# A decoder layer on one core: V's remainder and the router's logits ahead of the moments, the norm behind the maxima's copy, and one product less

## The chip, the cores and the metric

The kernel runs on one core of a Trainium2 chip. The metric is the device time of one execution in microseconds (us), the median of several runs. The core has five engines that work side by side, each through its own instructions in a fixed order: TensorE (PE; its weight loads are listed as PEld), VectorE (DVE), ScalarE (ACT), GpSimd (POOL) and SyncE (SP, which here issues the DMAs). They wait for each other by semaphores only.

## What is computed

A post-norm decoder layer over 128 sequences of 64 tokens of width 128, with 16 heads of 8. The core of the reference:

```python
x = layernorm(x + retention(x))            # decayed scores, no softmax, gate, norm
x = layernorm(x + cross_attention(x, ctx)) # softmax over 64 context rows
o = causal_self_attention(x)               # softmax over the earlier tokens
h = layernorm(x + o @ w_o, g1, b1)
probs = softmax(h @ wg)                    # router over 8 experts
topv, topi = top_k(probs, 2)
y = layernorm(h + sum of the two chosen experts' gelu MLPs, g2, b2)
```

## The kernel before

The 8192 tokens are 64 tiles of 128 rows (two sequences each), and four tiles make a group. Each group goes through the three attentions one after the other, so there are 48 groups in one stream, numbered g: 0 to 15 are retention, 16 to 22 are cross-attention, then self-attention (odd g) and cross-attention (even g) alternate up to 41, and 42 to 47 are self-attention. Groups from 16 on are the "later groups" of the change.

The program is written out slot by slot. Slot s belongs to group g = s // 4 with k = s % 4, and in every slot `pe_slot`, `act_slot`, `pool_slot` and `dve_slot` append what each engine has to do. That order is final, so an instruction that waits holds up all behind it on its engine. In one slot the engines serve groups of several ages. With g the group that the slot is named for:

- k = 2 and k = 3 project K and Q of g (L546, L549) into `bankA`. ACT copies them as `kh` (L670) and `qh` (L677), and DVE keeps the remainders `kl` and `ql` (L820). ACT also spreads `kh` into eight key blocks `Kz` (L686), four at k = 2 and four at k = 3.
- k = 3 computes V of g in `bankB` (L622). ACT copies it to half precision, `Vh` (L699, `act_values`), and DVE takes the remainder `Vl` (L832, `dve_values`). Before the change both stand at k = 0 of the next group.
- In every slot PE makes scores for one tile in row order (L449, L464), from which DVE takes the maximum of each row, `mx` (L814), and scores for an older tile in column order (L449, L486), of which ACT takes the exponential, `P` (L725). POOL computes the rounding remainder `Plo` (L766), and PE sums P with V (L509 to L511). In every second slot DVE divides the sums by the denominators and stores `O` (L851, L863).
- k = 0: "the maxima's turn". PE turns the maxima of g - 2 with four small products into `bankB` (L592), ahead of which stands `pe_keep_clock(bankB, 1)`, a 128x512 product of no use (L442). ACT copies the turned maxima out, `mT` (L706, `act_maxima`, written at k = 1).
- k = 1: PE turns `O` of g - 4 in the same `bankB` (L516). k = 2: ACT copies it (`OT`, L714) and PE multiplies it by the output weights (L611). k = 3: DVE adds the residual (L883).
- The norm at the end of a group: DVE takes the moments `st` and `mv` (L870, L874), POOL makes `rstd` and `nmr` of them (L772 to L777, `pool_rescale`), and ACT scales the rows (L731, `act_normalise`). For a self-attention group the moments are taken at k = 3 of the fourth group after it, and `pool_rescale` and `act_normalise` stand at k = 0 of the fifth. DVE then applies g1 and b1 (L888, L890, `dve_affine`), and the router reads the rows from the sixth group on: `dve_router` (L904, L908) frees `bankA` for the K projection. POOL sends the routed rows out by indirect DMA (L784), two per slot.

PE may not begin to turn `O` until `mT` is copied, since both use `bankB`:

```python
if begun(g - 2) and kind(g - 2) != "ret":
    pe.wait_ge(*f_mTs(softmaxed(g - 2)))
```

The functions that the diff touches, and those that call them:

Of the kernel before, what the change touches and what calls it, by code (L numbers as in the profile page):

```python
# [104 lines left out]
def build(nc, x, xt, ctxt, wmats, cols, rows, const_ident, const_masks, const_ids, const_tri, const_rev, const_steps, const_blocks, const_region, const_pads, const_rows, wg, w1, bb1t, w2, bb2, out):  # L105
# [214 lines left out]
    LS, LT, LP = 5, 10, 12  # L320
# [38 lines left out]
    def softmaxed(g):  # L359

        return g - NG
# [5 lines left out]
    def begun(g):  # L367
        return 0 <= g < GROUPS

    def last(g):  # L370
        return begun(g) and kind(g) == "self"
# [66 lines left out]
    def pe_keep_clock(o, times):  # L438


        for _ in range(times):
            pe.matmul(o, ident[:, :], W[:, 0:4, :].rearrange("p w n -> p (w n)")[:, 0:o.shape[1]], start=True, stop=True)  # L442
# [139 lines left out]
    def pe_second(g, k):  # L582


        if k == 0 and begun(g - 2) and kind(g - 2) != "ret":
            m = softmaxed(g - 2)
            pe.wait_ge(*(f_Vl(g - 1) if begun(g - 1) else f_r(g - 5)))
            pe.wait_ge(*f_mTs(m - 1))
            pe_keep_clock(bankB, 1)
            pe.wait_ge(*f_max(GT * m + GT - 1))  # L590
            for t in range(GT):
                i = pe.matmul(bankB[0:32, t * P:(t + 1) * P], mx[m % 2][:, t, :], ident16[:, :], start=True, stop=True)  # L592
            i.then_inc(f_mT.of(m), 1)
        if k == 1 and begun(g - 4):
            if begun(g - 1):
                pe.wait_ge(*(f_V32 if kind(g - 1) == "ret" else f_Vl)(g - 1))
            else:
                pe.wait_ge(*f_r(g - 5))
            if begun(g - 2) and kind(g - 2) != "ret":
                pe.wait_ge(*f_mTs(softmaxed(g - 2)))  # L600
            if kind(g - 4) == "ret":
                pe.wait_ge(*f_On(g - 4))
            else:
                pe.wait_ge(*f_O(2 * (g - 4) + 1))
            pe_turn(bankB, O[g % 2]).then_inc(f_OT.of(g - 4), 1)
        if k == 2 and begun(g - 4):
            pe.wait_ge(*f_OTs(g - 4))
            if kind(g - 4) == "ret":
                pe.wait_ge(*f_OTg(g - 4))
            for t in range(GT):  # L610
                i = pe.matmul(bankB[:, t * P:(t + 1) * P], OT[g % 2][:, t * P:(t + 1) * P], weights_of(g - 4)["O"],  # L611
                              start=True, stop=True)
            i.then_inc(f_out.of(g - 4), 1)
        if k == 3 and begun(g):
            if begun(g - 1):
                pe.wait_ge(*f_Vl(g - 1))
            if begun(g - 2) and kind(g - 2) != "ret":
                pe.wait_ge(*f_mTs(softmaxed(g - 2)))
            if begun(g - 4):
                pe.wait_ge(*f_r(g - 4))  # L620
            for t in range(GT):
                i = pe.matmul(bankB[:, t * P:(t + 1) * P], source_of(g)[:, t * P:(t + 1) * P], weights_of(g)["V"],  # L622
                              start=True, stop=True)
            i.then_inc(f_V.of(g), 1)
# [55 lines left out]
    def act_key_blocks(g, slots):  # L680
        m = softmaxed(g)
        if m >= 2:
            act.wait_ge(*f_S(GT * (m - 2) + GT - 1))
        act.wait_ge(*f_kh(g))
        for slot in slots:
            i = act.activation(Kz[g % 2][:, slot, :], kh[g % 2][:, :], ACT.Identity, scale=column(f"slot{slot}"))  # L686
        return i
# [45 lines left out]

    def act_slot(s):
        g, k = s // GT, s % GT
        if k == 0 and begun(g - 1):
            act_values(g - 1)
        if k == 1 and begun(g - 2) and kind(g - 2) != "ret":
            act_maxima(g - 2)
        if k == 2 and begun(g - 4):  # L740
            act_turned(g - 4)
        if k == 1 and CHOSEN.get(g, NG) < NG:
            act_turned_rows(CHOSEN[g])
        if begun(g):
            act_first(g, k)
        if NG * GT <= s - LT < TILES:
            act_weights(s - LT)
        if 0 <= s - LP < NG * GT and (s - LP) % 2:
            results(act, s - LP)
        if k == 2 and begun(g) and kind(g) != "ret":  # L750
            act_key_blocks(g, range(0, 4))
        if k == 3 and begun(g) and kind(g) != "ret":
            act_key_blocks(g, range(4, 8)).then_inc(f_Kz.of(softmaxed(g)), 1)
        if k == 0 and begun(g - 4) and kind(g - 4) == "ret":
            act_normalise(0, g - 4, O[g % 2]).then_inc(f_On.of(g - 4), 1)
        if k == 0 and begun(g - 6) and not last(g - 6):
            act_normalise(1, g - 6, tiles_of(g - 6)).then_inc(f_y.of(g - 6), 1)
        if k == 0 and last(g - 5):
            act_normalise(1, g - 5, tiles_of(g - 5)).then_inc(f_y.of(g - 5), 1)


# [25 lines left out]
    def pool_slot(s):  # L787
        g, k = s // GT, s % GT
        if k == 1 and begun(g) and kind(g) != "self":
            pool.wait_ge(*(l_x(g) if kind(g) == "ret" else f_xT(softmaxed(g))))  # L790
            pool.tensor_tensor(tiles_of(g), tiles_of(g), brow("a_bo" if kind(g) == "ret" else "x_bo"), ALU.add).then_inc(f_xb.of(unmasked(g)), 1)
        if k == 2 and begun(g - 4) and kind(g - 4) == "ret":
            pool.wait_ge(*f_OTs(g - 4))
            pool.tensor_tensor(OT[g % 2][:, :], OT[g % 2][:, :], gate[(g - 4) % 5][:, :], ALU.mult).then_inc(f_OTg.of(g - 4), 1)
        if k == 0 and last(g - 5):
            pool_rescale(1, g - 5)
        if k == 0 and begun(g - 4) and kind(g - 4) == "ret":
            pool_rescale(0, g - 4)
        if 0 <= s - LT < TILES:
            pool_low(s - LT)  # L800
        if k == 2 and begun(g - 5) and not last(g - 5):
            pool_rescale(1, g - 5)
        if s in PLACED:
            pool_dispatch(*PLACED[s])
# [137 lines left out]

    def dve_slot(s):
        g, k = s // GT, s % GT
        if k == 0 and begun(g - 1) and kind(g - 1) != "ret":
            dve_values(g - 1)
        if k == 3 and begun(g - 4):
            dve_residual(g - 4)
        if NG * GT <= s - LS < TILES:
# [8 lines left out]
            dve_low(g, f_kh, l_K(g - 2), kl, kh, {"ret": "a_bk", "cross": "x_bk", "self": "k_zero"}[kind(g)], f_kl)  # L958
        if NG * GT <= s - LP < TILES and (s - LP) % 2:
            results(dve, s - LP)  # L960

        if k == 1 and begun(g - 5) and not last(g - 5):
            dve.wait_ge(*f_r(g - 5))
# [6 lines left out]
            dve_scalars(0, g - 3, O[(g - 3) % 2])  # L970
        if s == GT * AT["self", 0]:
            dve_routing_constants()
        if k == 1 and last(g - 5) and s - LP < TILES:
            dve_affine(g - 5)
        if k == 1 and g in CHOSEN:
            dve_router(CHOSEN[g])
        if k == 1 and last(g - 5) and s - LP >= TILES:
            dve_affine(g - 5)
        if k == 2 and CHOSEN.get(g, NG) < NG:
            dve_choose(CHOSEN[g], 0)  # L980
        if k == 0 and CHOSEN.get(g - 1, NG) < NG:
            dve_choose(CHOSEN[g - 1], 1)

# [520 lines left out]
```

## Time and profile before

| | |
|---|---|
| median of three runs | 1338.22 us (1336.91 to 1345.8) |
| profiled execution | 1334.23 us, its span 1332.9 us |
| retention alone, 0 to 240 us | PE busy 190.65 us |
| later groups, 240 to 874 us | PE busy 535.23, DVE 463.85, ACT 463.06, POOL 422.92 us |
| experts and the rest, 874 us to the end | PE busy 346.79 us |
| TensorE clock, 240 to 874 us | 0.87 of full |

The span begins with the first instruction in the trace and ends with the last; the profiled execution's own time is 1.3 us more. All times on the trace are counted from the start of the span. The clock column is a share of full speed: 1.00 is the level of 2.4 GHz all the time, 0.50 is 1.2 GHz all the time. In a timeline row the brackets at the end give how long the engine sat idle before the row and what ended that. "issue" stands there where the profile shows no releaser.

### The profile page before, as it was taken

To read this page: it belongs to the slowest core of one execution; us is meant where nothing else is said; L and a number is where in the kernel's file an instruction comes from. 1 tells how busy PE (TensorE), PEld (TensorE's weight loads), DVE (VectorE), ACT (ScalarE), POOL (GpSimd) and SP (SyncE) were. 2 spreads that over 40 slices of the span, in tenths; PEclk is the share of its full clock that TensorE was granted. 3 is DMA by queue.
4 is the path that set the end of the run, shared out by engine and by line. 5 is a ranking of instruction groups with operands and counts; after the bars stand their busy time and mean duration, and the time that the engine had idled before them with its cause. 6 is when DMAs were issued, how large, how long until landed. Compare 5 with 4: busy or idle time off the path is not lost.

```text
span 1332.9 us, 45920 instructions
## 1 busy us (share of the span) xinstructions
PE 1072.7 (80%) x17677; PEld 758.1 (57%) x17677; DVE 891.3 (67%) x2322; ACT 821.9 (62%) x1884; POOL 911.8 (68%) x859
## 2 busy tenths in 40 slices
PE   5888888889898887887887788867788799999552
PEld 2555555545555554554554455546777789989210
DVE  4776767767877887677775676755445467666475
ACT  2455555788989876767766675424445456666366
POOL 4888888776666557766666665875657656667576
PEclk9998999888999988889987898758889899999776
DMA  5464332212222222222221212111212233332353
GB/s 159 128 188 144 86 82 75 58 49 73 77 81 79 67 66 71 69 59 58 81 69 50 74 37 68 49 39 42 57 55 69 61 88 105 97 95 67 119 166 103
DMA packets 132182, 108.61 MB, mean 81 GB/s; under 512 B 19564, under 2 KB 122477, under 8 KB 131933
## 3 DMA queue, kind: packets, MB, share of 16 engines
q1 hardware_dynamic: 123548, 88.29, 24.2%
q0 software_dynamic: 8416, 17.38, 4.0%
q8 instruction: 141, 2.31, 0.8%
q14 instruction: 77, 0.62, 0.2%
HBM read 41.58 MB, written 26.75 MB: 51 GB/s over the span
## 4 chain that ended last, share of the span: by engine, by line
PE 44%; ACT 17%; issue 13%; DVE 13%; DMA 5%; POOL 3%; SPq 2%; another core or an unknown queue 1%; DVEq 1%; ACTq 0%; POOLq 0%
PE bank L1213 7%; PE bank L1204 6%; ACT Kz L686 6%; PE bank L546 4%; PE bank L442 4%; PE bank L611 3%; PE bank L549 3%; DMA xrow<-block_rows 2%; PE bank L449 2%; PE bank L486 2%; DVE st L870 2%; DVE P L838 2%; DMA y_t<-expert_rows 2%; PE bank L516 2%; PE bank L509 2%
## 5 line engine op out<-in xcount | busy, mean ns | idle before, releaser
L766 POOL TENSOR_TENSOR Plo<-P 128x1024 f16<-128x1024 f32 x192 | 364.1, 1897 | 194.7 <-ACT P L725 165.8
L1256 POOL DMA_INDIRECT expert_rows<-yo,ix x135 | 172.9, 1281 | 106.4 <-DVE ix L1250 70.3
L1227 ACT ACTIVATE G<-bank,we 128x128 f32<-128x128 f32 x540 | 154.4, 370 | 98.6 <-PE bank L1204 72.1
L814 DVE TENSOR_REDUCE mx<-bank 128x16 f16<-128x1024 f32 x128 | 156.8, 1225 | 38.3 <-PE bank L464 36.5
L1213 PE MATMUL bank<-we,G 128*128 128x128 f32 x1080 | 150.3, 284 | 17.4 <-ACT G L1227 11.9
L686 ACT ACTIVATE Kz<-kh,col 128x512 f16<-128x512 f16 x256 | 163.2, 714 | 0.1
L784 POOL DMA_INDIRECT block_rows<-xs,slots x128 | 135.3, 1057 | 37.1 <-issue 36.5
L1204 PE MATMUL bank<-hTb,we 128*128 128x128 f32 x1080 | 149.3, 283 | 8.1 <-ACT hTb L1220 8.1
L509 PEld LDWEIGHTS bank<-Vh,P 64*128 64x128 bf16 x3072 | 124.4, 94 | 45.8 <-issue 30.7
L509 PE MATMUL bank<-Vh,P 64*128 64x17 f16 (+1 forms) x3072 | 146.1, 170 | 5.3 <-issue 4.9
L725 ACT ACTIVATE P<-bank 128x1024 f32<-128x1024 f32 x128 | 130.9, 1023 | 29.4 <-PE bank L486 24.6
L511 PE MATMUL bank<-Vl,P 64*128 64x16 f16 x3072 | 143.6, 167 | 6.4 <-issue 6.2
L1213 PEld LDWEIGHTS bank<-we,G 128*128 128x128 f32 x1080 | 136.3, 198 | 20.4 <-ACT G L1227 14.2
L510 PE MATMUL bank<-Vh,Plo 64*128 64x17 f16 (+1 forms) x3072 | 143.1, 168 | 4.7 <-issue 4.5
L1204 PEld LDWEIGHTS bank<-hTb,we 128*128 128x128 f32 x1080 | 137.1, 199 | 9.3 <-ACT hTb L1220 8.9
L1238 DVE COPY we<-wx 128x1156 f32 x135 | 103.9, 769 | 56.9 <-issue 48.6
L510 PEld LDWEIGHTS bank<-Vh,Plo 64*128 64x128 f16 x3072 | 126.6, 95 | 5.6 <-issue 5.1
L511 PEld LDWEIGHTS bank<-Vl,P 64*128 64x128 bf16 x3072 | 126.0, 94 | 5.9 <-issue 5.7
L486 PEld LDWEIGHTS bank<-Qz,Kst 64*64 64x64 f16 x3072 | 62.3, 116 | 88.8 <-issue 63.8
L442 PE MATMUL bank<-W,ident 128*128 128x256 f32 (+1 forms) x192 | 86.2, 534 | 31.9 <-DVE Vl L832 31.7
L731 ACT ACTIVATE xs<-xs,nmr,rstd 128x128 f32<-128x128 f32 x192 | 78.8, 488 | 48.8 <-POOL nmr L777 48.8
L486 PE MATMUL bank<-Qz,Kst 64*64 64x128 f16 x3072 | 85.8, 235 | 26.9 <-DVE P L838 25.5
(190 smaller groups left out, 2193.3 us busy)
## 6 DMA issues: line engine op xcount, KB each, us to landing
Qz<-qh SPq DMA_DIRECT2D x192, 64.0 KB
Kst<-kh SPq DMA_DIRECT2D x192, 64.0 KB, 2.0
xrow<-block_rows SPq DMA_DIRECT2D x135, 65.0 KB
y_t<-expert_rows SPq DMA_DIRECT2D x16, 512.0 KB, 4.3
Qz<-ql SPq DMA_DIRECT2D x96, 64.0 KB
Kst<-kl SPq DMA_DIRECT2D x96, 64.0 KB, 2.0
xT<-xt SPq DMA_DIRECT2D x16, 256.0 KB, 3.0
xs<-x SPq DMA_DIRECT2D x16, 256.0 KB, 3.2
```

The source lines that it names most:

```text
L442: pe.matmul(o, ident[:, :], W[:, 0:4, :].rearrange("p w n -> p (w n)")[:, 0:o.shape[1]], start=True, stop=True)
L486: i = pe.matmul(bank[64 * b:64 * b + 64, T_BANK + r, j * P:(j + 1) * P], Kst[g % 2][64 * r:64 * r + 64, j, at:at + S], Qz[g % 2][64 * r:64 ...
L509: pe.matmul(o, up[rows_b, cs], Vh[g % 3][rows_b, t, c, 0:nv], start=True, stop=False)
L510: pe.matmul(o, lo[rows_b, cs], Vh[g % 3][rows_b, t, c, 0:nv], start=False, stop=False)
L511: i = pe.matmul(o[:, 0:2 * DH], up[rows_b, cs], Vl[g % 3][rows_b, t, c, :], start=False, stop=True)
L686: i = act.activation(Kz[g % 2][:, slot, :], kh[g % 2][:, :], ACT.Identity, scale=column(f"slot{slot}"))
L766: pool.tensor_tensor(Plo[n % 3][:, :], P32[n % 3][:, :], upper(n), ALU.subtract).then_inc(f_Pl.of(n), 1)
L814: dve.tensor_reduce(columns, bank[:, S_BANK:S_BANK + 2, :].rearrange("p r (j i k) -> p r j i k", i=2, k=S), AX_X, ALU.max, negate=True).th ...
L1204: i = pe.matmul(bank[:, 2 + p, c * P:(c + 1) * P], we[b][:, W1 + c * P:W1 + (c + 1) * P], hTb[p][:, :], start=True, stop=True)
L1213: i = pe.matmul(bank[:, 4 + p, 0:P], G[b][:, c, :], we[b][:, W2 + c * P:W2 + (c + 1) * P], start=c == 0, stop=c == FC - 1)
L1227: i = act.activation(G[b][:, c, :], bank[:, 2 + p, c * P:(c + 1) * P], ACT.Gelu_apprx_tanh, bias=we[b][:, B1 + c:B1 + c + 1])
L1256: pool.indirect_dma_start(ydst[:, :], bass.IndirectOffsetOnAxis(ix2[s % 4][:, :], 0), yo[s % 4][:, :], None).then_inc(b_sc.of(s), 16)
```

## The change

In later groups V's copy and remainder move from k = 0 of the next group to k = 3 of the group itself: ACT copies `Vh` between its sixth and seventh key block, and DVE takes `Vl` ahead of the moments. `dve_router` moves ahead of the moments at k = 1. For a self-attention group ACT's norm moves from k = 0 to k = 1 (behind `act_maxima`), POOL's `pool_rescale` goes behind `pool_low` in the same slot, and `dve_affine` moves from k = 1 to k = 3. The product of no use in front of the maxima's turn goes. In the rows of the order below, line numbers of the changed file are one lower on ACT and one higher on DVE than before, for the same code.

```diff
--- before.py
+++ after.py
@@ -586,7 +586,6 @@
             m = softmaxed(g - 2)
             pe.wait_ge(*(f_Vl(g - 1) if begun(g - 1) else f_r(g - 5)))
             pe.wait_ge(*f_mTs(m - 1))
-            pe_keep_clock(bankB, 1)
             pe.wait_ge(*f_max(GT * m + GT - 1))
             for t in range(GT):
                 i = pe.matmul(bankB[0:32, t * P:(t + 1) * P], mx[m % 2][:, t, :], ident16[:, :], start=True, stop=True)
@@ -733,7 +732,7 @@
 
     def act_slot(s):
         g, k = s // GT, s % GT
-        if k == 0 and begun(g - 1):
+        if k == 0 and begun(g - 1) and kind(g - 1) == "ret":
             act_values(g - 1)
         if k == 1 and begun(g - 2) and kind(g - 2) != "ret":
             act_maxima(g - 2)
@@ -750,12 +749,14 @@
         if k == 2 and begun(g) and kind(g) != "ret":
             act_key_blocks(g, range(0, 4))
         if k == 3 and begun(g) and kind(g) != "ret":
-            act_key_blocks(g, range(4, 8)).then_inc(f_Kz.of(softmaxed(g)), 1)
+            act_key_blocks(g, range(4, 6))
+            act_values(g)
+            act_key_blocks(g, range(6, 8)).then_inc(f_Kz.of(softmaxed(g)), 1)
         if k == 0 and begun(g - 4) and kind(g - 4) == "ret":
             act_normalise(0, g - 4, O[g % 2]).then_inc(f_On.of(g - 4), 1)
         if k == 0 and begun(g - 6) and not last(g - 6):
             act_normalise(1, g - 6, tiles_of(g - 6)).then_inc(f_y.of(g - 6), 1)
-        if k == 0 and last(g - 5):
+        if k == 1 and last(g - 5):
             act_normalise(1, g - 5, tiles_of(g - 5)).then_inc(f_y.of(g - 5), 1)
 
 
@@ -792,12 +793,12 @@
         if k == 2 and begun(g - 4) and kind(g - 4) == "ret":
             pool.wait_ge(*f_OTs(g - 4))
             pool.tensor_tensor(OT[g % 2][:, :], OT[g % 2][:, :], gate[(g - 4) % 5][:, :], ALU.mult).then_inc(f_OTg.of(g - 4), 1)
-        if k == 0 and last(g - 5):
-            pool_rescale(1, g - 5)
         if k == 0 and begun(g - 4) and kind(g - 4) == "ret":
             pool_rescale(0, g - 4)
         if 0 <= s - LT < TILES:
             pool_low(s - LT)
+        if k == 0 and last(g - 5):
+            pool_rescale(1, g - 5)
         if k == 2 and begun(g - 5) and not last(g - 5):
             pool_rescale(1, g - 5)
         if s in PLACED:
@@ -942,8 +943,6 @@
 
     def dve_slot(s):
         g, k = s // GT, s % GT
-        if k == 0 and begun(g - 1) and kind(g - 1) != "ret":
-            dve_values(g - 1)
         if k == 3 and begun(g - 4):
             dve_residual(g - 4)
         if NG * GT <= s - LS < TILES:
@@ -958,6 +957,10 @@
             dve_low(g, f_kh, l_K(g - 2), kl, kh, {"ret": "a_bk", "cross": "x_bk", "self": "k_zero"}[kind(g)], f_kl)
         if NG * GT <= s - LP < TILES and (s - LP) % 2:
             results(dve, s - LP)
+        if k == 3 and begun(g) and kind(g) != "ret":
+            dve_values(g)
+        if k == 1 and g in CHOSEN:
+            dve_router(CHOSEN[g])
 
         if k == 1 and begun(g - 5) and not last(g - 5):
             dve.wait_ge(*f_r(g - 5))
@@ -970,14 +973,10 @@
             dve_scalars(0, g - 3, O[(g - 3) % 2])
         if s == GT * AT["self", 0]:
             dve_routing_constants()
-        if k == 1 and last(g - 5) and s - LP < TILES:
-            dve_affine(g - 5)
-        if k == 1 and g in CHOSEN:
-            dve_router(CHOSEN[g])
-        if k == 1 and last(g - 5) and s - LP >= TILES:
-            dve_affine(g - 5)
         if k == 2 and CHOSEN.get(g, NG) < NG:
             dve_choose(CHOSEN[g], 0)
+        if k == 3 and last(g - 5):
+            dve_affine(g - 5)
         if k == 0 and CHOSEN.get(g - 1, NG) < NG:
             dve_choose(CHOSEN[g - 1], 1)
 
```

On ACT around the maxima's turn of group 34, from k = 3 of group 33 to k = 2 of group 34, there stands before:

```order
L686 ACTIVATE Kz<-kh,col 128x512 x4
L699 CAST Vh<-bank 128x32x16
L662 COPY xT<-bank 128x512
L725 ACTIVATE P_0<-bank 128x1024
L731 ACTIVATE xs<-xs,nmr,rstd 128x128 x8
L706 CAST mT<-bank 32x512
L725 ACTIVATE P_1<-bank 128x1024
L714 ACTIVATE OT<-bank,col 128x512
L670 ACTIVATE kh<-bank,col 128x512
```

and with the change:

```order
L685 ACTIVATE Kz<-kh,col 128x512 x2
L698 CAST Vh<-bank 128x32x16
L685 ACTIVATE Kz<-kh,col 128x512 x2
L661 COPY xT<-bank 128x512
L724 ACTIVATE P_0<-bank 128x1024
L730 ACTIVATE xs<-xs,nmr,rstd 128x128 x4
L705 CAST mT<-bank 32x512
L724 ACTIVATE P_1<-bank 128x1024
L730 ACTIVATE xs<-xs,nmr,rstd 128x128 x4
L713 ACTIVATE OT<-bank,col 128x512
L669 ACTIVATE kh<-bank,col 128x512
```

Of the eight scalings in a row, the four of the self-attention group have moved behind `mT` and the next `P`, right in front of `OT`; the `Vh` copy has moved ahead of two key blocks.

On DVE at k = 3 of group 33 and k = 0 of group 34 (`st` and `mv` are the moments, `mx` the row maxima that PE turns next) there stands before:

```order
L851 RECIPROCAL rden<-bank 128x32
L863 TENSOR_TENSOR O<-bank,rden 64x16x8 x4
L870 BN_STATS st<-xs 128x6 x4
L874 BN_AGGR mv<-st 128x2 x4
L832 TENSOR_TENSOR Vl<-bank,Vh 128x512
L814 TENSOR_REDUCE mx<-bank 128x8x2
```

and with the change:

```order
L852 RECIPROCAL rden<-bank 128x32
L864 TENSOR_TENSOR O<-bank,rden 64x16x8 x4
L833 TENSOR_TENSOR Vl<-bank,Vh 128x512
L871 BN_STATS st<-xs 128x6 x4
L875 BN_AGGR mv<-st 128x2 x4
L815 TENSOR_REDUCE mx<-bank 128x8x2
```

`Vl` and the moments have changed places; the last maximum stands behind both, as before.

On DVE one group later, from k = 1 of group 34 to k = 0 and 1 of group 35 (the `xs<-xs,row` rows are `dve_affine`, `xs<-bank,xs` the residual), there stands before:

```order
L863 TENSOR_TENSOR O<-bank,rden 64x16x8 x4
L888 TENSOR_TENSOR xs<-xs,row 128x4x128
L890 TENSOR_TENSOR xs<-xs,row 128x4x128
L814 TENSOR_REDUCE mx<-bank 128x8x2
L820 SCALAR_TENSOR_TENSOR kl<-bank,col,kh 128x512
L883 TENSOR_TENSOR xs<-bank,xs 128x4x128
L814 TENSOR_REDUCE mx<-bank 128x8x2
L820 SCALAR_TENSOR_TENSOR ql<-bank,col,qh 128x512
L851 RECIPROCAL rden<-bank 128x32
L863 TENSOR_TENSOR O<-bank,rden 64x16x8 x4
L832 TENSOR_TENSOR Vl<-bank,Vh 128x512
L814 TENSOR_REDUCE mx<-bank 128x8x2 x2
```

and with the change:

```order
L864 TENSOR_TENSOR O<-bank,rden 64x16x8 x4
L815 TENSOR_REDUCE mx<-bank 128x8x2
L821 SCALAR_TENSOR_TENSOR kl<-bank,col,kh 128x512
L884 TENSOR_TENSOR xs<-bank,xs 128x4x128
L815 TENSOR_REDUCE mx<-bank 128x8x2
L821 SCALAR_TENSOR_TENSOR ql<-bank,col,qh 128x512
L852 RECIPROCAL rden<-bank 128x32
L864 TENSOR_TENSOR O<-bank,rden 64x16x8 x4
L833 TENSOR_TENSOR Vl<-bank,Vh 128x512
L889 TENSOR_TENSOR xs<-xs,row 128x4x128
L891 TENSOR_TENSOR xs<-xs,row 128x4x128
L815 TENSOR_REDUCE mx<-bank 128x8x2 x2
```

The two affine steps have moved from k = 1 to stand between `Vl` and the maximum that the next turn waits for.

## Rows read from the trace of the kernel before

**Rows 1.** Windows: busy us of each engine, clock share of full, DMA.
```profile
374.00:466.00 92.00, 80.67 (x1934) 51.32 (x1926) 74.83 (x172) 80.51 (x131) 57.23 (x52) 1.00 0.29 78
...
480.00:860.00 380.00, 315.32 (x6172) 192.47 (x6170) 270.50 (x655) 250.09 (x401) 251.75 (x226) 0.85 0.23 63
...
550.00:558.00 8.00, 7.95 (x94) 4.49 (x94) 3.40 (x5) 5.32 (x8) 7.18 (x7) 0.50 0.44 120
```

**Rows 2.** Waits: engine, line, releaser: us total, times, longest.
```profile
PEld bank L442 <- DVE Vl L832: 34.7, 31, 2.3
...
PE bank L516 <- issue: 24.0, 10, 3.1
...
PE bank L546 <- DVE lg L908: 13.9, 10, 1.9
```

**Rows 3.** Groups of instructions by shape, 280 to 880 us: busy, mean ns, idle before.
```profile
L442 PE MATMUL bank<-W,ident 128*128 128x512 f32 x62 | 40.6, 741 | 30.2 <-DVE Vl L832 30.2
...
L516 PE MATMUL bank<-ident,O 128*128 128x128 f32 x124 | 24.9, 335 | 24.0 <-issue 24.0
```

**Rows 4.** Timeline of PE, groups 34 and 35: start, length, instruction.
```profile
543.10 1.13 PE L442 MATMUL bank<-W,ident 128*128 128x512 f32 x2 [0.56 <-DVE Vl L832]
544.24 0.40 PE L592 MATMUL bank<-ident,mx 128*32 128x128 f16 x4
...
550.05 1.08 PE L516 MATMUL bank<-ident,O 128*128 128x128 f32 x4 [3.10 <-issue]
...
555.38 2.07 PE L611 MATMUL bank<-W,OT 128*128 128x128 f32 x8
...
565.15 1.55 PE L442 MATMUL bank<-W,ident 128*128 128x512 f32 x2 [1.07 <-DVE Vl L832]
566.63 0.61 PE L592 MATMUL bank<-ident,mx 128*32 128x128 f16 x4
```

**Rows 5.** Timeline of ACT, the same two groups.
```profile
547.85 1.65 ACT L731 ACTIVATE xs<-xs,nmr,rstd 128x128 f32<-128x128 f32 x4 [3.08 <-POOL nmr L777]
549.40 0.56 ACT L706 CAST mT<-bank 32x512 f16<-32x512 f32 x1
...
554.24 0.69 ACT L670 ACTIVATE kh<-bank,col 128x512 f16<-128x512 f32 x1 [2.31 <-PE bank L546]
...
559.86 0.69 ACT L677 ACTIVATE qh<-bank,col 128x512 f16<-128x512 f32 x1 [1.59 <-PE bank L549]
...
561.35 2.55 ACT L686 ACTIVATE Kz<-kh,col 128x512 f16<-128x512 f16 x4
563.80 0.58 ACT L699 CAST Vh<-bank 128x512 f16<-128x512 f32 x1
```

**Rows 6.** Timeline of POOL, start of group 34.
```profile
547.61 0.20 POOL L777 TENSOR_TENSOR nmr<-mv,rstd 128x4 f32<-128x4 f32 x1
547.76 1.89 POOL L766 TENSOR_TENSOR Plo<-P 128x1024 f16<-128x1024 f32 x1
```

**Rows 7.** Timeline of DVE, around the turn of group 34.
```profile
541.03 0.87 DVE L870 BATCH_NORM_STATS2 st<-xs 128x6 f32<-128x128 f32 x4
...
542.36 0.69 DVE L832 TENSOR_TENSOR Vl<-bank,Vh 128x512 f16<-128x512 f32 x1
542.96 1.22 DVE L814 TENSOR_REDUCE mx<-bank 128x16 f16<-128x1024 f32 x1
...
549.53 0.69 DVE L888 TENSOR_TENSOR xs<-xs,row 128x512 f32<-128x512 f32 x1 [0.88 <-ACT xs L731]
550.25 0.69 DVE L890 TENSOR_TENSOR xs<-xs,row 128x512 f32<-128x512 f32 x1
```

**Rows 8.** Timeline of ACT, group 26, where no self-attention group ends yet.
```profile
402.42 1.65 ACT L731 ACTIVATE xs<-xs,nmr,rstd 128x128 f32<-128x128 f32 x4
403.96 0.56 ACT L706 CAST mT<-bank 32x512 f16<-32x512 f32 x1
```

**Rows 9.** Timeline of PE, the same group.
```profile
405.09 0.66 PE L516 MATMUL bank<-ident,O 128*128 128x128 f32 x4
...
408.33 1.16 PE L611 MATMUL bank<-W,OT 128*128 128x128 f32 x8
```

## The prediction, made before the change was run

> **What bounds the kernel now.** I read four views in this order: the windows, to see which stage the change touches; the list of waits, for who stops there; the timelines of PE, ACT, POOL and DVE over one pair of later groups (34, whose k = 0 carries a self-attention norm, and 35, whose k = 0 carries none); and the same for a group early in the stage. The change touches only the later groups. In all of 480 to 860 us PE is busy for 315 of 380 us, and its clock is at 0.85 of full, so that some 30% of that time runs at 1.2 GHz; from 374 to 466 us it is at 1.00 throughout [rows 1]. No engine is full: each waits for the next one in turn, and what counts is the loop of waits.
>
> In group 34 that loop reads so. DVE takes the moments, then `Vl`, then the last maximum, which ends at 542.96 + 1.22 = 544.18 [rows 7]. PE starts the useless product at `Vl`'s end and turns the maxima at 544.24 [rows 4]. The next thing that PE wants in `bankB` is to turn `O`, and it starts at 550.05, after 3.10 us idle. The profile names no releaser ("issue"), but `mT` ends at 549.96 [rows 5], and the code makes PE wait for it. `mT` itself stood behind four scalings, which waited 3.08 us for POOL's `nmr` [rows 5], ready at 547.81 [rows 6]. There are ten such stalls, 24.0 us together, 3.1 the longest [rows 2]. Where PE has stood still, its clock is lower: from 550 to 558 us it is granted 0.50 of full, the 1.2 GHz level [rows 1].
>
> Group 35 waits elsewhere: on DVE's `Vl`, held up by ACT's last two key blocks (`Vh` starts at 563.80, [rows 5]); then in the K projection for the router's logits, ten times, 13.9 us in all [rows 2].
>
> **The useless product** costs 1.13 us each time at full clock, 31 of them, 40.6 us of PE busy time [rows 3, 4]. I count its removal at nothing by itself. In group 34 the maximum ends at 544.18 and the product at 544.24: it fills a wait of the same length, since DVE begins the 1.22 us maximum when it has finished `Vl`. Only what pulls DVE forward moves this turn. The cover has a cost when gone: PE idles 0.56 + 1.13 = 1.7 us in front of the turn, and the clock may fall there (below).
>
> **`Vl` ahead of the moments, group 34.** DVE does the same work up to the maximum, in another order: `O`, moments 1.33 us (541.03 to 542.36), `Vl`, maximum [rows 7]. The end stays at 544.18. Nothing gained, nothing lost at this turn.
>
> **`Vh` ahead of two key blocks, and affine moved.** In groups like 35 `Vh` comes two blocks earlier, 2 x 2.55/4 = 1.27 us [rows 5]. But `dve_affine` now stands between `Vl` and the maximum: 549.53 to 550.94, 1.41 us [rows 7]. The two cancel to 0.14 us lost at that turn. At k = 1, where the affine stood, DVE was waiting anyway (0.88 us before it).
>
> **`mT` ahead of the norm.** With the maxima turned at 544.64, `mT` can start when ACT has finished the four scalings of the cross-attention group, which stay ahead of it: it ends at about 545.4, not 549.96. PE then goes on from its sums without the 3.1 us. This is not all gain, because the norm now stands in front of `OT` and `kh`. POOL computes `Plo` first, so `nmr` is ready 1.89 us later, at 547.81 + 1.89 = 549.7 [rows 6]. ACT scales until 549.7 + 1.65 = 551.4, copies `OT` until about 552.0 and starts `kh` at 552.1 instead of 554.24 [rows 5]: 2.1 us earlier. PE has by then done its products of k = 2 and waits up to some 1.8 us in front of L611. From `kh` to `Vh` ACT took 563.80 - 554.24 = 9.56 us, of which 1.59 was the wait for Q [rows 5] and 1.27 the two blocks now behind. Since Q's turn comes no later relative to `kh`, 6.7 us are left: `Vh` at 558.8. Then 0.6 for `Vh`, 0.7 `Vl`, 1.4 affine and 1.2 maximum: PE turns the maxima at 562.7, against 566.63 [rows 4]. That is 3.9 us for a stall of 3.10. Eight of the ten stalls are of this kind (1.75 to 3.12 us, 22 of the 24.0 us), so 22 x 3.9/3.1 = 27.7; I take 27. The lower bound is what `kh` alone gains, 8 x 2.1 = 17, the upper one 8 x 3.9 = 31 and one us for each of the two short stalls.
>
> **Router ahead of the moments.** In the ten waits of the K projection DVE's moments (1.33 us each) are the last thing ahead of the logits, so at most 10 x 1.33 = 13 us. Half the time something else will be late by then (PE's own router products and `O` turns), so 6, with bounds 0 and 13.
>
> **Groups 18 to 27** have no self-attention norm and no affine, so `Vh` 1.27 us earlier does pull `Vl`, the maximum and the turn. But ACT's order up to `mT` holds no more slack: `mT` starts when the four scalings end (403.96, [rows 8]) and ends at 404.5, and PE turned `O` at 405.09 [rows 9]. The gain is 405.09 - 404.52 = 0.57 us per group, 6 us for ten, with bounds 0 and 12.
>
> **The clock.** What it costs is read at both levels: from `O`'s turn to the output product PE took 408.33 - 405.09 = 3.2 us at full clock [rows 9] and 555.38 - 550.05 = 5.3 at half [rows 4], 2.1 us per group. In groups with the norm that is hidden behind `nmr` now. In the ten groups like 35 it is not, but PE idles 1.07 + 1.1 us there even before any change, filled by the product, so new low stretches are likely in some. I take two or three of them, 5 us; bounds 0 and 22 x 2.1 = 46 (the 32 turns but the ten that have the stall already). The Trainium skill ("TensorE: Matmul & The Clock Gate", A second HAM failure mode: psum-queue depth-cycling) says that short idle times between groups of products, repeated, make the clock swing between its levels. By that rule a product removed from a wait is no free product; the trace agrees so far that the clock is at 0.50 after the stall [rows 1].
>
> **Sum.** -27 - 6 - 6 + 5 = -34 us. Against the profiled execution of 1334.2 that is 1300.2; the median of the three runs lies 4.0 above it, so I predict 1338.2 - 34 = 1304 us. Retention and the expert stage do not change; the five last groups, whose norm waits lie in front of `mT` too, are left at nothing.
>
> **Rivals.** (a) *The wait only moves.* ACT's norm in front of `OT`, plus affine on DVE's path, take back nearly all: `kh` gains 2.1 in eight groups (17), affine takes 1.4 in ten (14), the logits find PE or DVE still late: some -3, with the early groups' 6 about -9, 1329 us. For it speaks that in the early groups ACT is busy 80.5 of 92 us and DVE 74.8 [rows 1], so that a group pulled forward soon meets a full engine; against it, that the 1.59 us and 1.27 us on ACT are real slack, and that from 480 to 860 us ACT is busy for only 250 of 380 us and DVE for 270. Chance 0.14. (b) *The clock decides.* Without the product PE's clock is low after nearly every turn of the maxima. The price is the bound above, 46 us, and the gain shrinks to 17 + 6 + 6 = 29 because ACT waits for a slow PE: +17, 1355 us. It decides against the change from 14 of the 22 groups on. For it: idle of 1.7 to 2.2 us at each turn; against it, that the stage from 374 to 466 us, with a product and a wait at each turn too, held full clock [rows 1], and that in the early groups the idle time in front of the turn does not grow, because product and 1.27 us leave together. Chance 0.08. (c) *More comes than I count*: stalls and the low clock behind them vanish together in all eight groups, and L611 to L549 run at full clock too (2.1 us more in each of eight groups, the router's full 13): about 1280. Chance 0.13. (d) *The change does not do what it says*: no sign, the order shows each move. The forecast has the rest, 0.65.
>
> **Range and chances.** A measurement of this kernel can tell about 1% (13 us) from no change. The forecast's own terms span 1290 to 1322; the range reaches to (a) and most of (c): 1280 to 1335. Faster by over 1% (below 1325): the forecast, (c), and a bit of (a), 0.80. Within 1%: most of (a), 0.12. Slower: 0.08.
>
> **What would show it.** After the change the ten waits of PE L516 on "issue" should be nearly gone, `mT` should end within 1.2 us of the turn, and a wait for POOL's `nmr` should stand in front of the scalings just before `OT`. PE should idle 1.5 to 2.3 us in front of the maxima's turn, released by DVE's maximum. The K projection should hardly wait for `lg`. Between 480 and 860 us the clock should be near 0.85 or above; below 0.75 means (b). From the turn of a group like 34 to the next there were 566.63 - 544.24 = 22.4 us; there should be 18.5 to 19.5. Wrong would be the case that PE's wait before L611 grows to the full 3 us, or that DVE turns out to be full between the turns.

## The result, and the profile after

The changed kernel takes 1354.27 us (median of five runs, 1351.32 to 1364.06), the kernel before 1343.16 us in the same comparison. The ratio is 1.011, with a 95% interval of 1.0064 to 1.0155: slower by about 1%, where 2.6% faster was forecast. Measured a second time, on another chip, it was 1360.05 against 1341.65 us, ratio 1.0132 (1.0087 to 1.0177). Ratios, here and below, leave out single executions more than 1.5% above the fastest of the same kernel, so they can differ a little from the quotient of the two medians.

The windows of the changed kernel, to be read against [rows 1]:

```profile
374.00:466.00 92.00, 79.20 (x1839) 51.35 (x1838) 69.36 (x158) 78.66 (x129) 57.43 (x51) 0.88 0.28 77
480.00:860.00 380.00, 326.21 (x6119) 204.22 (x6119) 277.48 (x636) 258.27 (x411) 246.51 (x225) 0.72 0.22 63
562.00:566.00 4.00, 3.66 (x81) 2.33 (x80) 3.93 (x4) 1.60 (x2) 3.81 (x5) 0.50 0.36 106
...
240.00:874.00 634.00, 538.80 (x10723) 340.86 (x10717) 460.11 (x1053) 459.81 (x760) 408.94 (x373) 0.76 0.23 65
```

From 374 to 466 us the granted clock was 1.00 and is 0.88; from 480 to 860 us it was 0.85 and is 0.72. Over the whole of the later groups, 240 to 874 us, it falls from 0.87 to 0.76, while PE is busy for much the same time as before (538.8 against 535.23 us): it does less work in it. The 0.72 is below the 0.75 that the prediction had set as the sign of its rival (b).

The signs that the prediction had set for the moves themselves came. Waits of the changed kernel, against [rows 2]:

```profile
PE bank L591 <- DVE mx L815: 61.4, 32, 4.2
...
ACT xs L730 <- POOL nmr L778: 15.5, 9, 2.1
...
PE bank L516 <- issue: 7.6, 9, 1.1
```

The wait in front of `O`'s turn (PE L516 on "issue") is down from 24.0 us to 7.6, the longest from 3.1 to 1.1. But PE now waits 61.4 us for DVE's maximum, in front of each of its 32 turns, and ACT's norm waits for `nmr` where it now stands. The wait of the K projection for the router's logits (13.9 us in [rows 2]) is gone. The timeline of PE over groups 34 and 35, against [rows 4]:

```profile
561.43 0.58 PE L591 MATMUL bank<-ident,mx 128*32 128x128 f16 x4 [2.13 <-DVE mx L815]
...
564.54 1.11 PE L516 MATMUL bank<-ident,O 128*128 128x128 f32 x4
...
567.15 2.08 PE L546 MATMUL bank<-cT,W 128*128 128x512 f32 x2
...
570.63 1.16 PE L610 MATMUL bank<-W,OT 128*128 128x128 f32 x8
...
581.20 0.59 PE L591 MATMUL bank<-ident,mx 128*32 128x128 f16 x4 [0.86 <-DVE mx L815]
```

The maxima are turned at 561.43 and `O` at 564.54, 3.1 us after the turn and not 5.8. But `O`'s turn takes 1.11 us and the K projection 2.08: the 1.2 GHz level (clock 0.50 from 562 to 566 us, in the windows above), from the turn on. From turn to turn there are 581.20 - 561.43 = 19.8 us, where I had forecast 18.5 to 19.5 and the kernel before had 22.4. This group gained 2.6 us. Its neighbour lost: the group before it, whose turn is at 540.59 us, needs 20.8 us against 19.0, and all through 480 to 700 us each group now takes 19.7 to 21.0 us, whether it carries a norm or not. Added up from turn to turn, groups 18 to 27 take 165.0 us against 158.0, groups 28 to 41 take 281.2 against 271.9, and only groups 42 to 48 gain, 152.1 against 156.5.

ACT and DVE at the same place, against [rows 5] and [rows 7]:

```profile
562.11 0.57 ACT L705 CAST mT<-bank 32x512 f16<-32x512 f32 x1 [0.68 <-PE bank L591]
...
566.54 1.65 ACT L730 ACTIVATE xs<-xs,nmr,rstd 128x128 f32<-128x128 f32 x4 [1.60 <-POOL nmr L778]
568.10 0.67 ACT L713 ACTIVATE OT<-bank,col 128x512 f32<-128x512 f32 x1
569.33 0.69 ACT L669 ACTIVATE kh<-bank,col 128x512 f16<-128x512 f32 x1 [0.56 <-issue]
...
577.07 0.59 ACT L698 CAST Vh<-bank 128x512 f16<-128x512 f32 x1
```

```profile
560.08 1.20 DVE L815 TENSOR_REDUCE mx<-bank 128x16 f16<-128x1024 f32 x1
...
562.07 2.57 DVE L933 TENSOR_TENSOR chosen<-rev,r 128x32 bf16<-128x32 f32 x1
...
577.69 0.69 DVE L833 TENSOR_TENSOR Vl<-bank,Vh 128x512 f16<-128x512 f32 x1
578.29 0.89 DVE L889 TENSOR_TENSOR xs<-xs,row 128x512 f32<-128x512 f32 x1
579.22 0.69 DVE L891 TENSOR_TENSOR xs<-xs,row 128x512 f32<-128x512 f32 x1
579.83 1.22 DVE L815 TENSOR_REDUCE mx<-bank 128x16 f16<-128x1024 f32 x1
```

On ACT `mT` ends 0.67 us behind the turn's last product (5.3 us before), the norm waits 1.60 us for `nmr` right in front of `OT`, and `kh` comes 7.9 us after the turn instead of 10.0: the 2.1 us of the prediction. On DVE one row is new: the router's `chosen` takes 2.57 us, where its like took 0.19 (544.98 us in the trace before). That is the first sign of a cost that the prediction did not have.

### The profile page after: what moved, and what is told of

Same layout as the page of the kernel before. It is cut to its first block, busy times and chain, and to the rows that moved or that the text cites. A ratio compares the mean times of both kernels' runs of the same rounds, so it can differ in the third digit from the quotient of the medians.

```text
span 1354.3 us, 45821 instructions
## 1 busy us (share of the span) xinstructions
PE 1089.1 (80%) x17613; PEld 779.1 (58%) x17613; DVE 901.4 (67%) x2322; ACT 825.1 (61%) x1884; POOL 910.3 (67%) x859
## 4 chain that ended last, share of the span: by engine, by line
PE 47%; DVE 15%; ACT 15%; issue 12%; DMA 5%; POOL 3%; another core or an unknown queue 2%; SPq 1%; DVEq 0%; ACTq 0%; POOLq 0%
PE bank L1203 7%; PE bank L1212 7%; PE bank L546 6%; ACT Kz L685 4%; PE bank L610 3%; DVE mx L815 3%; PE bank L516 3%; PE bank L486 3%; PE bank L549 3%; PE bank L449 2%; PE bank L464 2%; DMA xrow<-block_rows 2%; DVE P L839 2%; DMA y_t<-expert_rows 2%; DVE st L871 2%
## 5 line engine op out<-in xcount | busy, mean ns | idle before, releaser
L685 ACT ACTIVATE Kz<-kh,col 128x512 f16<-128x512 f16 x256 | 167.0, 717 | 0.1
L486 PEld LDWEIGHTS bank<-Qz,Kst 64*64 64x64 f16 x3072 | 65.3, 122 | 97.3 <-issue 73.3
L486 PE MATMUL bank<-Qz,Kst 64*64 64x128 f16 x3072 | 91.2, 246 | 26.8 <-DVE P L839 25.7
L1243 DVE TENSOR_TENSOR yo<-bank,we 128x128 f32<-128x128 f32 x135 | 39.1, 289 | 63.5 <-PE bank L1212 40.5
```

Of the source, the lines that this page charges most:

```text
L486: i = pe.matmul(bank[64 * b:64 * b + 64, T_BANK + r, j * P:(j + 1) * P], Kst[g % 2][64 * r:64 * r + 64, j, at:at + S], Qz[g % 2][64 * r:64 ...
```

## Experiments

Each kernel was run 6 to 12 times beside the kernel before on the same chip. The chips of the sessions differ (before took 1303, 1339 and 1342 us on them), so times are compared as ratios to it. The last two columns come from the one profiled execution of each kernel: "clock" is the granted clock from 240 to 874 us, and "turns" is the time from the first turn of the maxima to the last of the 32, the stretch in which the change acts. It is 586.4 us in the kernel before and 598.3 in the changed one; e12, the same kernel as the latter, is 4 us from it. Such a time comes from one execution. The whole time of that execution was 9 to 11 us below its kernel's median for the kernel before, e6 and e10, and 10 to 16 us above for e8, e9 and e11, so differences of a few us in this column say nothing.

| run | what it is | us | before | ratio (95%) | clock | turns |
|---|---|---|---|---|---|---|
| e1 | change, product back | 1290.69 | 1303.06 | 0.9869 (0.981 to 0.9929) | 0.87 | 567.4 |
| e2 | before, product out | 1327.05 | 1303.06 | 1.0185 (1.0145 to 1.0224) | 0.78 | 596.3 |
| e3 | change, two products | 1281.2 | 1303.06 | 0.9834 (0.9792 to 0.9876) | 0.91 | 552.4 |
| e4 | before, norm, rescale, affine moved | 1315.24 | 1303.06 | 1.0097 (1.0065 to 1.0128) | 0.85 | 596.6 |
| e5 | e1, affine ahead of Q's remainder | 1309.49 | 1338.7 | 0.9796 (0.9756 to 0.9836) | 0.88 | 561.7 |
| e6 | before, V and router moved | 1313.06 | 1338.7 | 0.9809 (0.9766 to 0.9852) | 0.87 | 556.4 |
| e7 | before, two products | 1346.57 | 1338.7 | 1.0075 (1.0045 to 1.0105) | 0.91 | 586.9 |
| e8 | e5, two products | 1311.83 | 1338.7 | 0.9797 (0.9763 to 0.9831) | 0.91 | 571.7 |
| e9 | e1, affine back at k = 1 | 1300.96 | 1341.65 | 0.9685 (0.9641 to 0.9729) | 0.88 | 554.9 |
| e10 | e9, two products | 1305.71 | 1341.65 | 0.9736 (0.9695 to 0.9777) | 0.90 | 554.5 |
| e11 | change, half a product | 1331.29 | 1341.65 | 0.9944 (0.9911 to 0.9977) | 0.82 | 578.3 |
| e12 | the change again | 1360.05 | 1341.65 | 1.0132 (1.0087 to 1.0177) | 0.76 | 602.5 |

**e1, the product put back.**

```diff
             pe.wait_ge(*f_mTs(m - 1))
+            pe_keep_clock(bankB, 1)
             pe.wait_ge(*f_max(GT * m + GT - 1))
```

> The changed kernel with the product of no use put back in front of the maxima's turn, nothing else. Theory C (the clock): the missing product is the whole loss; the other moves are worth what the prediction gave them, about -39 us without its clock term, so some 1304 to 1315 us, with the granted clock from 240 to 874 us back at 0.85 or above (0.76 in the changed kernel, 0.87 before). Rival M (the moves): the norm in front of OT and the affine on DVE's path lose as much as mT gains, and the clock only follows; then about 1345 to 1354 us.

0.9869: the one line turns 1% slower into 1.3% faster, and the clock is back at 0.87. So the product is the reason for the loss (theory C). But the gain stops at 1.3%, 17 us of the 39 that the moves should bring (by the plain medians of this noisy kernel, 12 us); C had asked for more. Its trace shows where some of it is. DVE, POOL and PE of this kernel in front of one turn:

```profile
638.69 0.69 DVE L834 TENSOR_TENSOR Vl<-bank,Vh 128x512 f16<-128x512 f32 x1
639.30 2.68 DVE L890 TENSOR_TENSOR xs<-xs,row 128x512 f32<-128x512 f32 x1
642.01 2.27 DVE L892 TENSOR_TENSOR xs<-xs,row 128x512 f32<-128x512 f32 x1
644.20 1.22 DVE L816 TENSOR_REDUCE mx<-bank 128x16 f16<-128x1024 f32 x1
```

```profile
636.69 0.96 POOL L786 DMA_INDIRECT block_rows<-xs,slots  x1 [0.30 <-issue]
637.67 6.05 POOL L768 TENSOR_TENSOR Plo<-P 128x1024 f16<-128x1024 f32 x3
```

```profile
640.42 1.13 PE L442 MATMUL bank<-W,ident 128*128 128x512 f32 x2
645.48 0.61 PE L592 MATMUL bank<-ident,mx 128*32 128x128 f16 x4 [3.92 <-DVE mx L816]
```

The two affine steps, 0.69 us each in [rows 7], take 2.68 and 2.27 us while POOL makes three remainders `Plo` one after the other (3 x 1.89 = 5.7 us alone, 6.05 here). PE waits 3.92 us for the maximum behind them. The affine steps end at 641.98 and 644.28 us, each some 0.6 us behind the end of one of POOL's three (641.42 and 643.73, the single rows merged above).

The groups of this trace differ among themselves. In groups 32, 34, 38 and 40 both steps are long (2.24 to 2.68 us), and such a group and the next take 41.9 to 42.8 us from turn to turn, the second of them at a clock of 0.71 to 0.79. In group 36 both are short, and the pair takes 37.7 us, group 37 at full clock. So a part of what the long steps cost seems to come by the clock of the group behind them. The waits of e1 also show one that the prediction named as the sign of its own error:

```profile
PE bank L592 <- DVE mx L816: 41.6, 23, 4.3
...
PE bank L611 <- ACT OT L714: 12.1, 6, 2.9
```

With the product back, PE stops in front of the output product for ACT's `OT`, six times and up to 2.9 us (once, 1.9 us, in the kernel before): some of the stall has moved there, as rival (a) of the prediction said.

**e2, only the product taken out of the kernel before** (the same line with a minus, in the kernel before).

> The kernel before without that product, nothing else. Theory C: the low clock comes without any of the moves, so 1365 to 1390 us (before 1343, plus about 40), clock from 240 to 874 us near 0.76. Rival M: the product only fills a wait, so within 5 us of before, clock near 0.87.

1.0185, that is 24 us slower without any of the moves. This is the cleanest test of the step that failed. The windows row of this kernel:

```profile
240.00:874.00 634.00, 519.55 (x10680) 329.94 (x10684) 459.23 (x1063) 454.90 (x759) 412.62 (x377) 0.78 0.23 65
```

The clock is 0.78 where it was 0.87. The size is less than the 40 us that C expected, and by the turns it is only 10 us (596.3 against 586.4, of traces from two chips).

**e3, e11 and e7, more or less of the product.** e3 has `pe_keep_clock(bankB, 2)`, e11 `pe_keep_clock(bankB[:, 0:256], 1)` in the change; e7 has two in the kernel before.

> The changed kernel with two such products at that place. The wait for DVE's maximum behind them was 1.7 us or more by the prediction, one product takes 1.13 us, so a second one sticks out by some 0.5 to 1 us per group (32 groups: 15 to 30 us) if only time on PE counts. Theory C: part of that comes back by a higher clock, so within 10 us of the run with one product. Rival M: 15 to 30 us above it.

> The changed kernel with a product of half the columns (256, some 0.5 us) at the turn. Theory C as a matter of amount: between none (1.011) and one (0.987), ratio 0.995 to 1.003, clock from 240 to 874 us between 0.76 and 0.87. Rival: any work in the gap will do; ratio 0.987.

> The kernel before with two products instead of one. The first is hidden behind DVE's maximum (1.13 us against 1.22), so the second, 1.13 us, is on PE's way in each of 32 groups: +36 us if only time counts, ratio 1.027. Theory C (the clock pays): a third or more comes back, ratio 1.00 to 1.017.

In the change, none, half, one and two products give ratios of 1.0132, 0.9944, 0.9869 and 0.9834, with clocks of 0.76, 0.82, 0.87 and 0.91. Half a product gives back 1.9%, on one chip and clear of noise (0.995 to 1.003 had been expected). The next two steps, 0.75% for the other half (measured on another chip) and 0.35% for a second whole one, are not clear of noise by themselves, since their intervals overlap; the clock and the turns (602.5, 578.3, 567.4, 552.4 us) go the same way at each step. So the amount of work in the gap counts, not only that there is some. In e7 the second product should take 1.13 us of PE's way in 32 groups, 36 us, and costs 10 (0.75%). The clock went up from 0.87 to 0.91, which may have paid the rest; how much of the second product lay in a wait was not measured.

**e12, the change itself beside e9 to e11.**

> The changed kernel itself, on the chip of these runs, so that none, half and one product can be compared. Ratio 1.006 to 1.016 as measured before, clock near 0.76 from 240 to 874 us.

1.0132 and 0.76, as expected. So none and half a product are compared on one chip, one and two products on another.

**e4, the norm's moves alone.**

```diff
-        if k == 0 and last(g - 5):
+        if k == 1 and last(g - 5):
             act_normalise(1, g - 5, tiles_of(g - 5)).then_inc(f_y.of(g - 5), 1)
# pool_rescale(1, g - 5) behind pool_low, dve_affine(g - 5) from k == 1 to k == 3, as in the change
```

> The kernel before with one part of the change: ACT's norm behind the maxima's copy, POOL's rescale behind its remainder, the affine steps at k = 3. The product stays; V's parts and the router stay where they were. Theory C: the stall of 3.1 us goes, worth 27 us by the prediction less 1.4 us of affine in ten groups that V's earlier copy no longer makes up, so 1318 to 1330 us, clock above 0.87. Rival M: 1340 us or more, because the wait moves in front of OT.

1.0097: the stall of 3.1 us is gone (PE L516 on "issue": 1.0 us in all) and the kernel is 1% slower. By its size that is rival M, but the wait that M names is too small for it: PE waits 8.1 us for `OT`, where it was 1.9. What both theories lacked is the length of the affine steps. By shape, from 280 to 880 us:

```profile
L888 DVE TENSOR_TENSOR xs<-xs,row 128x512 f32<-128x512 f32 x12 | 25.6, 2131 | 0.3
...
L890 DVE TENSOR_TENSOR xs<-xs,row 128x512 f32<-128x512 f32 x12 | 18.2, 1514 | 0.4
```

43.8 us for twelve groups, where [rows 7] would give 12 x 1.4 = 17, all of it in front of the maximum for which PE waits. The clock has a part in it too, though the product is in place: in groups 32 to 40 of even number PE idles 5.7 to 7.5 us from turn to turn (2.7 to 4.6 before), and the group behind each runs at a clock of 0.74 to 0.77 (0.77 to 0.95 before). No run takes the two apart.

**e6, the other part alone**: V's parts and the router as in the change; norm, rescale and affine as before.

> The kernel before with the other part of the change: V's copy and remainder at k = 3 ahead of the moments, the router ahead of the moments. The product stays, the norm, POOL's rescale and the affine steps stay where they were. By the prediction's terms: 6 (early groups) + 6 (router) + up to 13 (V's copy 1.27 us earlier in ten groups, with no affine in its way), so 12 to 25 us, ratio 0.98 to 0.99. Rival: the stall in front of O's turn takes all of it back in the ten groups that have it, because DVE is early but ACT's copy of the maxima still waits; then ratio 0.99 to 1.0.

0.9809, 25.6 us faster, at the top of the expected 12 to 25 and not at the rival's. Waits of this kernel:

```profile
PE bank L516 <- issue: 32.0, 21, 3.1
...
PE bank L592 <- DVE mx L816: 12.2, 13, 1.2
```

PE's wait in front of `O`'s turn is longer than before (32.0 us) and the kernel gains all the same. The affine steps stayed at 0.69 us in nearly all groups. From the turn of group 34 to the next there are 19.0 us, inside the 18.5 to 19.5 that the prediction had worked out from the norm's moves, and here the norm is where it was.

**e5 and e8, the affine steps in another place.**

```diff
+        if k == 3 and last(g - 5):
+            dve_affine(g - 5)
         if k == 3 and begun(g):
             dve_low(g, f_qh, l_Q(g - 2), ql, qh, ...)
...
-        if k == 3 and last(g - 5):
-            dve_affine(g - 5)
```

> The changed kernel with the product back, and the affine steps at k = 3 moved from behind V's remainder to between the slot's maximum and the remainder of Q, where POOL is sending rows and not computing. In the run with the product back these steps took up to 2.68 and 2.27 us in the groups in which they ran beside POOL's remainder of P, not 0.69 each. Theory P (they wait for POOL): both steps are back at 0.69 us and the time is 1.0 to 1.5% below that run (ratio to before 0.972 to 0.977, where that run had 0.987). Rival: the length comes from the rows themselves or from PE's delay; then the ratio stays at 0.987.

> As the run with the affine steps ahead of Q's remainder, with two products at the maxima's turn. Two products over one gained 0.35% where DVE was late; with DVE earlier the second one is no longer hidden in all groups: ratio within 0.5% of the run with one product, 0.968 to 0.98. If the clock gains more than the product costs, it is the fastest version.

0.9796, against 0.9869 with the steps behind `Vl`; the intervals overlap. The place was badly chosen: in three groups the first step took even longer there, 4.43 to 4.92 us, with two of POOL's `Plo` beside it. The time alone neither shows nor refutes that the steps wait for POOL. e8, with two products, is the same (0.9797).

**e9 and e10, the affine steps back at k = 1.**

```diff
+        if k == 1 and last(g - 5):
+            dve_affine(g - 5)
         if k == 2 and CHOSEN.get(g, NG) < NG:
             dve_choose(CHOSEN[g], 0)
-        if k == 3 and last(g - 5):
-            dve_affine(g - 5)
```

> The changed kernel with one product back and the affine steps back at k = 1, behind the router and the moments. There POOL is sending rows, and DVE waits for ACT's norm of the same slot. Theory P (the affine steps beside POOL's remainder cost several us each): all steps at 0.69 us, the group pairs of 41 us at 35 to 38, ratio to before 0.965 to 0.975. Rival: the wait for the later norm at k = 1 holds up DVE's next maximum and the remainder of K as much as the collisions did; ratio 0.98 to 0.99.

> As the last one with two products at the turn. With DVE earlier, the second product is on PE's way; if the clock is near 1.00 already with one, it costs up to 1.1 us per group and the ratio is 0.5 to 1.5% higher; if the clock is still below 0.9 in the stage, it stays within 0.5%.

e9 gives 0.9685, the lowest ratio of all: 3.1% faster than the kernel before, and 1.8% better than e1 on ratios, the intervals apart, though the two were measured on two chips. Its affine steps and its wait for the maximum:

```profile
L890 DVE TENSOR_TENSOR xs<-xs,row 128x512 f32<-128x512 f32 x14 | 11.9, 850 | 12.1 <-issue 10.7 <-ACT xs L731 1.3
...
L892 DVE TENSOR_TENSOR xs<-xs,row 128x512 f32<-128x512 f32 x14 | 9.7, 693 | 0.5
```

```profile
PE bank L592 <- DVE mx L816: 12.8, 13, 1.2
```

The steps are back at 0.69 us (the mean of the first is raised by two groups at 1.8 us), and PE's wait for the maximum is 12.8 us, not the 41.6 us of e1. The pairs of groups from 32 to 41 take 37.8 to 41.0 us, and not the expected 35 to 38. DVE now idles in front of the steps, where the later norm is what it needs (12.1 us in all); that costs less. (The profiled execution of e9 took 1312.51 us, above the kernel's median.) A second product (e10, 0.9736) is 0.5% higher; the intervals overlap, so no difference is shown.

e9 differs from e6 only in the norm's moves: ACT's norm behind `mT`, and POOL's `pool_rescale` behind `Plo`. The ratios give them 0.9809 - 0.9685 = 1.2%, 17 us, over two sessions. The traces give them nothing: 556.4 us of turns against 554.9, and the first product of the experts starts at 879.3 us in e6 and at 879.7 in e9. They show a gain and a loss of one size. Groups 42 to 48 take 149.4 us in e6 and 136.2 in e9, but groups 28 to 41 take 249.3 and 262.7. The router's `chosen`, by shape from 280 to 880 us, first in e6, then in e9:

```profile
L934 DVE TENSOR_TENSOR chosen<-rev,r 128x32 bf16<-128x32 f32 x13 | 2.5, 192 | 0.5
L934 DVE TENSOR_TENSOR chosen<-rev,r 128x32 bf16<-128x32 f32 x13 | 14.9, 1145 | 0.5
```

With `pool_rescale` behind it, POOL's `Plo` now runs where DVE makes `chosen`, and the maximum behind that comes later: 578.69 and 2.40 us for `chosen`, beside a `Plo` from 579.12 to 581.03. That this is the loss of the alternating groups is read off the traces; no run moves `pool_rescale` by itself.

## Why the prediction was wrong, step by step

- **"I count its removal at nothing by itself", with +5 us in "The clock", is the step that failed.** The reading was right that the product hides behind the 1.22 us maximum. But its worth is not its place on PE's way; it keeps the clock. Taking it out costs 24 us in the kernel before (e2, 1.85%), and in the change the step from one product to none is 0.9869 to 1.0132, 2.6% or 35 us (two chips; the turns give 31 and 35 us). The mechanism was in the text as rival (b), with 1355 us at a chance of 0.08; the time came out at 1354.27. That the number fits so well is luck: (b) took 46 us for the clock and 29 for the moves, and it was 35 and about 17. My argument against it, that 374 to 466 us held full clock with a wait at each turn, was no argument: each of those waits had the product in it. The same stretch is at 0.88 now.
- **The bound of its price** (46 us, at 2.1 us for each of 22 groups) was fair; taking 5 of it was not. Idle time alone was my yardstick for where the clock falls. In e2, e11 and e3 only the amount of work in the gap changes, and the clock follows it.
- **"`mT` ahead of the norm", -27 us, is the largest term that failed beside it.** What was read off came: the stall is gone, and `kh` comes 2.1 us earlier. That this brings 3.9 us per group did not. With the affine steps in a harmless place the norm's moves bring some 17 us by the ratios and 1.5 us by the turns (e6 against e9), and in the even groups from 32 to 40, most of the eight for which the sum was made, the traces show a loss. What the sum left out is that `Plo` ahead of `nmr` meets `chosen` on DVE. Between 17 us and nothing the size stays open.
- **"Affine moved", 1.41 us.** The length was taken from a place where POOL sends rows, and used at a place where POOL computes. There the two steps took up to 5 us (e1) and 5.8 us (e4). With the product in, this costs 1.8% by the ratios (e1 against e9), 25 us, and 12.5 us by the turns; on the kernel before, norm and affine moved together lose 1% (e4). In the change itself it did not show (none of its affine steps is over 0.98 us), perhaps because the slow PE leaves POOL waiting for work; there `chosen` met POOL instead (20.6 us for all its rows from 280 to 880 us, 14.6 before).
- **V's parts and the router**, -12 us by the terms (-6 for groups 18 to 27, -6 for the router): e6 measured 25.6 us. Its trace shows it elsewhere than the terms had it: groups 18 to 27 gained 0.4 us, groups 28 to 41 22.6 (271.9 to 249.3). "Nothing gained" in group 34 was wrong; it went from 22.4 to 19.0 us. I gave the later groups nothing for the earlier `Vh`, since the affine steps cancel it; without them there, it counts.
- **The parts as measured**: -26 (e6), -17 (norm, e6 to e9), +25 (affine, e9 to e1), +35 (clock, e1 to e12) make +17 us. That this is the 18 us of e12 proves nothing: the four are the steps of one chain of ratios that ends at e12, so they add up to it whatever they are. Each is uncertain by 5 to 8 us, and the middle two are much smaller in the traces. What holds without the chain is the first and, from e2 alone, 24 us (19 to 29) for the product.

That the affine steps are long because they wait for POOL is shown as far as this. The 14 traces hold 448 affine steps. The 77 that are longer than 0.75 us all have a `Plo` beside them and end 0.55 to 0.56 us behind the end of one, and none that began with more than 0.15 us of a `Plo` to go is short. One `Plo` beside them is 2.35 us long instead of 1.89, and moved back to k = 1 they are short. POOL's work was not taken away to test it. The Trainium skill ("SBUF — State Buffer", SBUF: two separate sides) states the rule: VectorE and GpSimd share one pair of ports; of an instruction of VectorE with two SBUF inputs and one of GpSimd that reads SBUF, the one that starts first has the pair for its whole length, and the other waits. The traces agree that the two exclude each other: `Vl` and the maximum of the later groups, which read PSUM, keep their 0.69 and 1.20 to 1.24 us wherever a `Plo` runs beside them. In who goes first it is less simple: the step at 639.30 us came during one `Plo` and also had to wait for the whole of the next. The kernel before had the sign already: seven `chosen` rows of 1.60 to 1.66 us up to 880 us, where most others take 0.19 to 0.21, and an affine step of 2.27 us at 436.97.

What stays open is what in the product counts for the clock. Turns of `O` and sums of P and V are work on PE too, and they run in all these kernels.

## What to carry to other kernels

A product that looks useless inside a wait is to be priced by the granted clock, not by the time it covers: take it out alone, once, before building on its absence. A duration holds for the place where it was measured; before a VectorE step with two operands in SBUF is moved, look at what GpSimd does at the new place. And a change of several moves is better timed part by part, on one chip: here two parts were worth 3.1% together, and two others hid it.

## What the runs showed of the hardware

- With the same instructions otherwise and a 128x512 product in each of 32 gaps, the mean granted clock over 634 us went 0.76 (none), 0.82 (256 columns), 0.87 (one), 0.91 (two). PE's busy share hardly moved (538.84, 544.37, 529.80 and 548.16 of 634 us).
- VectorE's 128x512 step with both inputs in SBUF takes 0.69 us alone and up to 4.9 us beside GpSimd's `Plo`; a 128x32 step took up to 2.64 us (e4) instead of 0.19.
- The kernel before took 1303 us (median of 15 runs) on one chip and 1339 to 1343 us on the others, the same program. More than half of the difference lies in the expert stage, which no run here changes: from its first product to the end of the span there are 403 to 407 us in the traces e1 to e4, on the fast chip, and 420 to 435 in the others. The attention stage runs alike: groups 18 to 27 take the same time from turn to turn, to 0.1 us, in the kernel before and in e4. Why the expert stage differs is open.
